# Two elements innermost in place of four in the one-hot operands of a graph kernel's adjacency build

## The reference, cut to what matters

```python
agg = jax.ops.segment_sum(h[src], dst, num_segments=n)       # network 0, three times
z = jax.nn.relu(_batchnorm((h + agg) @ W1[i] + b1[i], g1[i], be1[i])) @ W2[i] + b2[i]
...
summed = jax.ops.segment_sum(x[col], row, num_segments=n)    # network 1: src and dst swapped, mean
msg_sum = jax.ops.segment_sum(x[src], dst, num_segments=n)   # network 2: mean
neigh = jax.ops.segment_max(feat[src] * w[:, None], dst, num_segments=N)   # network 3: maximum, then a weighted mean
```

## Time and profile before

| what | us |
|---|---|
| median of 3 runs | 4930.73 |
| lowest and highest of the 3 | 4900.83, 4937.73 |
| the profiled execution | 4922.53 |
| its span in the profile | 4920.7 |
| PE busy in the span | 3483.8 (71%) |
| DVE busy | 2147.8 (44%) |
| ACT busy | 1956.0 (40%) |
| GpSimd (POOL) busy | 1782.5 (36%) |

### The profile page before, as it was taken

One profiled execution on the slowest core, in us unless ns is written; L12 is line 12 of the kernel. 1 busy time (PEld: TensorE's weight loads), 2 busy tenths in 40 slices (PEclk: granted clock), 3 DMA queues, 4 the chain that ended last, 5 costly groups with the idle time before them and its releaser, 6 DMA issues.

```text
span 4920.7 us, 57973 instructions
## 1 busy us (share of the span) xinstructions
PE 3483.8 (71%) x22119; PEld 2928.1 (60%) x22119; DVE 2147.8 (44%) x4433; ACT 1956.0 (40%) x3073; POOL 1782.5 (36%) x1727
## 2 busy tenths in 40 slices
PE   4899999921112997995118999983477686877678
PEld 2677777611002996994108989973355565665566
DVE  7776676610001986884012233242233333333335
ACT  4677777710000444554005546552222222222221
POOL 3000000077773000777760000005555555556530
PEclk9999999955555998997559989996788898889889
DMA  4878788800002667442004424423255555556555
GB/s 146 228 213 230 214 219 231 240 21 7 7 7 47 223 236 236 151 130 53 4 7 140 133 72 144 130 62 108 71 196 185 193 189 191 188 197 214 170 183 179
DMA packets 299723, 712.84 MB, mean 145 GB/s; under 512 B 65270, under 2 KB 167445, under 8 KB 284214
## 3 DMA queue, kind: packets, MB, share of 16 engines
q1 hardware_dynamic: 167180, 436.77, 27.7%
q10 hardware_dynamic: 52298, 174.64, 9.9%
q0 software_dynamic: 79968, 97.68, 9.2%
HBM read 503.59 MB, written 254.50 MB: 154 GB/s over the span
## 4 chain that ended last, share of the span: by engine, by line
PE 53%; another core or an unknown queue 25%; DVE 7%; issue 6%; ACT 6%; DMA 2%; ACTq 1%; DVEq 0%; SPq 0%
PE PS L740 21%; PE PS L1725 7%; PE PS L662 6%; PE PS L625 5%; PE PS L1711 3%; PE PS L671 2%; PE PS L1701 2%; DMA turned<-DEG 2%; PE PS L1693 2%; DVE BB L1877 2%; ACT DEG L884 1%; PE PS L718 1%; ACT CA L859 1%; DVE PAN L549 1%
## 5 line engine op out<-in xcount | busy, mean ns | idle before, releaser
L431 POOL DMA_INDIRECT PAN<-table,src_i x832 | 826.6, 994 | 1359.1 <-DMA table<-DEG 769.7
L972 POOL DMA_INDIRECT shares<-dst_f,spare x832 | 886.7, 1066 | 738.1 <-ACTq L777 426.8
L740 PE MATMUL PS<-CX,XH 125*128 125x376 f32 x2000 | 477.8, 318 | 261.6 <-issue 181.2
L740 PE MATMUL PS<-CX,XL 125*128 125x376 f32 x2000 | 472.9, 315 | 141.9 <-issue 141.9
L740 PEld LDWEIGHTS PS<-CX,XH 125*128 125x128 f32 x2000 | 321.3, 197 | 279.9 <-issue 219.9
L1819 ACT ACTIVATE BB<-PS 128x1024 f32<-128x1024 f32 x104 | 106.5, 1024 | 938.5 <-PE PS L1701 567.6
L625 PE MATMUL PS<-hot 128*128 128x250 bf16 x1250 | 382.7, 397 | 34.7 <-ACT CA L859 20.3
L537 ACT ACTIVATE CX<-PAN 125x3125 fp32r<-125x3125 uint8 x106 | 298.2, 2815 | 271.1 <-PE PS L740 233.6
L740 PEld LDWEIGHTS PS<-CX,XL 125*128 125x128 f32 x2000 | 321.7, 197 | 141.5 <-issue 141.5
L740 PE MATMUL PS<-CP,XH 125*128 125x376 f32 (+1 forms) x1330 | 310.7, 313 | 120.3 <-DVE XL L1070 63.0
L1701 PE MATMUL PS<-ident,BB 128*128 128x128 f32 x832 | 141.5, 325 | 310.6 <-DVE BB L1877 249.6
(11 more groups left out here) (334 smaller groups left out, 6998.0 us busy)
## 6 DMA issues: line engine op xcount, KB each, us to landing
PAN<-counts SPq DMA_DIRECT2D x300, 390.6 KB
shares<-SSB ACTq DMA_DIRECT2D x70, 1600.0 KB
XP<-shares SPq DMA_DIRECT2D x50, 1600.0 KB
PAN<-shares SPq DMA_DIRECT2D x50, 1600.0 KB
BB<-start_penalty SPq DMA_DIRECT2D x104, 512.0 KB
shares<-blank ACTq DMA_DIRECT2D x15, 3200.0 KB, 13.7
turned<-DEG SPq DMA_DIRECT2D x50, 781.2 KB, 9.3
PAN<-turned SPq DMA_DIRECT2D x100, 390.6 KB
```

The lines of the kernel that those rows point to most:

```text
L431: nc.gpsimd.indirect_dma_start(out=gbuf[g % 2][:, k, :], out_offset=None, in_=source, in_offset=bass.IndirectOffsetOnAxis(ap=src_i[:, t:t ...
L740: last = nc.tensor.matmul(wide_ps[b][h][:, 0:w], halves[part][0:TN, s * SUBJ + j, :], cast_part(v, j, h), start=(s == 0 and j == 0 and par ...
L972: nc.gpsimd.indirect_dma_start(out=shares_flat, out_offset=bass.IndirectOffsetOnAxis(ap=share_at[:, t:t + 1], axis=0), in_=share[:, t:t + ...
```

## The change

`hot_lo` is stored as [2 pairs][128 values][2 windows] in place of [128][4], and `hot_key` as [4 windows][125 values][2 halves] in place of [2][125][4]. The counting table is repeated twice in place of four times. Sizes, instruction counts, waits and order stay as they were; PE reads both operands with a step of two bf16 elements, 4 bytes, and DVE's inputs repeat in runs of two elements.

```diff
-        hot_lo = [hot[:, r * hot_size:r * hot_size + QUAD * 128].rearrange("p (n w) -> p n w", w=QUAD) for r in range(RING)]
-        hot_key = [hot[:, r * hot_size + QUAD * 128:(r + 1) * hot_size].rearrange("p (a n w) -> p a n w", a=2, w=QUAD)
+        hot_lo = [hot[:, r * hot_size:r * hot_size + QUAD * 128].rearrange("p (q n w) -> p q n w", q=2, w=2) for r in range(RING)]
+        hot_key = [hot[:, r * hot_size + QUAD * 128:(r + 1) * hot_size].rearrange("p (w n a) -> p w n a", w=QUAD, a=2)
                    for r in range(RING)]
...
-        iota_h = firsts[:, 0:128 * QUAD].rearrange("p (n w) -> p n w", w=QUAD)
+        iota_h = firsts[:, 0:256].rearrange("p (n w) -> p n w", w=2)
...
-                    keys = hot_key[u % RING][:, i % 2, :, :].rearrange("p n (w a) -> p w a n", w=2)[:, x, :, :]
-                    last = nc.tensor.matmul(pair_ps[n % 2][:, x, :], hot_lo[u % RING][:, :, 2 * (i % 2) + x], keys,
+                    keys = hot_key[u % RING][:, 2 * (i % 2) + x, :, :].rearrange("p n a -> p a n")
+                    last = nc.tensor.matmul(pair_ps[n % 2][:, x, :], hot_lo[u % RING][:, i % 2, :, x], keys,
                                             start=True, stop=True)
...
-            placed_after(dve, nc.vector.tensor_copy(iota_h, iota[:, :].unsqueeze(2).to_broadcast([128, 128, QUAD])))
+            placed_after(dve, nc.vector.tensor_copy(iota_h, iota[:, :].unsqueeze(2).to_broadcast([128, 128, 2])))
...
-                nc.vector.tensor_tensor(out=hot_lo[r], in0=iota_h,
-                                        in1=slot_lo[:, w:w + QUAD].unsqueeze(1).to_broadcast([128, 128, QUAD]),
-                                        op=ALU.is_equal)
-                keys = slot_key[:, 2 * w:2 * w + 2 * QUAD].rearrange("p (a w) -> p a w", a=2)
+                los = slot_lo[:, w:w + QUAD].rearrange("p (q w) -> p q w", q=2)
+                nc.vector.tensor_tensor(out=hot_lo[r], in0=iota_h.unsqueeze(1).to_broadcast([128, 2, 128, 2]),
+                                        in1=los.unsqueeze(2).to_broadcast([128, 2, 128, 2]), op=ALU.is_equal)
+                keys = slot_key[:, 2 * w:2 * w + 2 * QUAD].rearrange("p (w a) -> p w a", w=QUAD)
                 nc.vector.tensor_tensor(out=hot_key[r],
-                                        in0=iota_h[:, 0:TN, :].unsqueeze(1).to_broadcast([128, 2, TN, QUAD]),
-                                        in1=keys.unsqueeze(2).to_broadcast([128, 2, TN, QUAD]),
+                                        in0=iota_h[:, 0:TN, :].unsqueeze(1).to_broadcast([128, QUAD, TN, 2]),
+                                        in1=keys.unsqueeze(2).to_broadcast([128, QUAD, TN, 2]),
                                         op=ALU.is_equal).then_inc(hot_full, 1)
```

## The result

The changed kernel took 4881.49 us on the median of 20 runs (4840.47 to 4909.2), the kernel before 4925.59 (4900.83 to 4960.68). The ratio is 0.9916, 95% interval 0.9898 to 0.9934: 41 us less (33 to 50) where 90 were forecast. The change is a gain, but less than half of the forecast. The median lies inside the range that the prediction gave (4795 to 4890), near its slow end.

What follows compares the result with a forecast made beforehand. PE was taken to bound the build (280 to 944.2 us). Gains of 86 there and 18 before, less 12 for late DMAs and 2 for the scatter's start, gave 90 us: 4930.7 to 4841 us, range 4795 to 4890 (0.81).

Steps and rivals of the forecast that it cites:

- Which engine bounds the build, and what L625 costs: Build: PE bounds it; a 4-byte step takes L625 from 0.22 to 0.11 us a product, 0.22 us less a pair.
- Rival (b): L625: a step of 4 bytes is no faster than 8, or the step wasn't the cause; no gain, 4931 us; chance 0.12.
- VectorE keeps its pairs: DVE's quads: runs of two still let L1168 handle two elements at a time; a quad stays at 1.06 us.
- rival (c): DVE's quads: pairing lost, a quad takes 1.86 us, kernel 57 us slower at 4988 us; chance 0.07.
- L1164 unchanged: DVE: a sign that the forecast is right, L1164 and L1168 keep their durations.
- Odd products, 37: Build's 7 odd products: 43.0 us becomes 37, PE, ACT and DVE coupled by two-buffer rings; gain 6 each (bounds 8.4 and 3).
- Even products, 39.4 and then 1.5 for DMA: Build's 8 even products: 44.9 us becomes 39.4, PE-bound; 1.5 each charged for late turned writes, 12 in all.
- Rival (a), DMA takes over: Build: DMA becomes the bound, even products gain only 1 us each, 66 us in all, 4865 us; chance 0.14.
- The beginning: Before 280 us: slice 0's pairs and products 0 to 3 gain 18 us in sum.
- The 38 pairs of slice 0: Before product 0: a ring of PE, ACT and PE; 0.2 us off each of 19 rounds, 4 us.
- The end: Scatter and everything behind it: starts near 890 us and keeps its length, so the kernel gains what the build gains.
- the DMA backlog: Between build and scatter: the scatter's start at 980.03 us hangs on it; 2 us more charged for a longer one.

Runs made afterwards that it cites:

- Experiment 3: Changed kernel with only the moving operand (the key's one-hot) at a step of two elements, the stationary one still at four; single execution 4854.8 us.
- experiment 7: Changed kernel with five DMAs for each turned tile and the stationary operand (source's one-hot) back in its old layout; 0.9792 of the kernel before, 4833.5 us.
- Experiment 6: Changed kernel with five DMAs for each turned tile, leaving out 831 of 832 edge-weight columns on VectorE (result incomplete); single execution 4810.3 us.
- experiment 1: Changed kernel with each turned tile written in five DMAs in place of one, each fifth waited for by itself; 0.9833 of the kernel before, 4825.7 us.
- experiment 2: Kernel before the change with the same five DMAs for each turned tile, each fifth waited for by itself; 0.9988 of the kernel before, 4896.1 us.
- experiment 5: Changed kernel, one DMA for each turned tile, with each even product's four zero writes moved from steps 10, 20, 30, 40 to 28, 35, 42, 49; single execution 4847.6 us.
- experiment 8: Changed kernel with five DMAs for each turned tile and product 19's three zero writes moved to products 5, 9 and 13; 0.9823 of the kernel before.

## Why the prediction was wrong

**Which engine bounds the build, and what L625 costs.** Right. The 0.44 us of a pair was the moving operand's step of 8 bytes, and 4 bytes cost nothing (a pair takes 0.23 us afterwards). Experiment 3 shows it by the operand alone, and 1250 products went from 402 to 278 ns. Rival (b) is out. The Trainium skill, "SBUF — State Buffer", section "Door 1", would have bf16 steps of 4 elements read free; as TensorE's moving operand they read at half speed here, and the measurement decides.

**VectorE keeps its pairs.** Right for L1168, 672 ns before and after, so rival (c) is out. "L1164 unchanged" was wrong by 67 ns, which experiment 7 shows without effect.

**Odd products, 37.** They came to 38.3, a gain of 4.7 each in place of 6, or 33 us in place of 42. The step named three engines in a ring. Experiment 6 strikes VectorE from it.

**Even products, 39.4 and then 1.5 for DMA: the step that failed.** "More writes are late. I charge 1.5 for each of the 8 even products (bounds 0 and 4.5 each)." The mechanism was the right one, in the right place, but the term measures 6.2, beyond its upper bound. With the late write the 8 even products take 369.4 us (the changed kernel), without it 320.1 (experiment 1), 49 over 8. Their sums, in this order:

```profile
sum 369.42, PE 329.06 PEld 253.84 DVE 254.79 ACT 264.77 POOL 7.34; mean PE 41.13 PEld 31.73 DVE 31.85 ACT 33.10 POOL 0.92
```

```profile
sum 320.13, PE 314.54 PEld 246.71 DVE 254.44 ACT 264.22 POOL 7.32; mean PE 39.32 PEld 30.84 DVE 31.80 ACT 33.03 POOL 0.92
```

ScalarE waits for the write once in each of the 8, 42.5 us together. PE stands 34.8 us longer for it (40.4 beside 5.6), and is busy 14.5 us longer for the same instructions, at the lower clock behind each stall. The forecast had no term for that second part. What it took off for the faster reads was right: 320.1 us is 5.5 a product less than the 364.1 before. The split itself is worth little of it, 2.0 us of these products in experiment 2.

How could it have been sized? That the time to reuse shrinks by 2 us was right (17.5 to 15.3). But the prediction held against it the median landing of 9.3 us and charged an average, while the same write is the slow one in every even product, since the schedule puts it beside the counts write each time. The trace before shows it landing in 15.5, 19.0, 20.2, 16.6 and 20.6 us. Against 15.3 these alone give an estimate of 3.1 us a product, twice the charge. The rest is the write's own slowing and the clock.

**Rival (a), DMA takes over.** It forecast 4865 by way of a full DMA. The time came nearer to it than to the forecast, but experiments 1 and 5 show that capacity wasn't short: the same bytes fit when they are waited for later or issued elsewhere.

**The beginning.** The first four products and what is before them gained 6.1 us in place of 18. The 38 pairs of slice 0 gained 0.8 (PE's first L662 at 89.0 in place of 89.9) in place of 4: the ring's round hardly shrank. Product 0 gained 5.6 beside a forecast of 5. Then product 1 grew from 57.2 to 62.2 and took it back. Its first copy into the tile CA waits until the counts write of slice 0 has landed, before and after the change:

```profile
140.32 1.16 ACT L859 ACTIVATE CA<-PS 128x500 bf16<-128x500 f32 x2 [3.11 <-DMA counts<-CA]
```

```profile
139.42 1.16 ACT L859 ACTIVATE CA<-PS 128x500 bf16<-128x500 f32 x2 [8.83 <-DMA counts<-CA]
```

Product 1 starts 6.4 us sooner and gets going 0.9 us sooner. Product 2 gained 0.5 in place of 5, with a wait of 3.9 for a `turned` write; in experiment 1 it takes 41.2, the 5 us. Product 3 gained 4.2.

**The end.** Product 19 and the scatter's start moved with the build (35.8 to 35.6), and the gain of the build reached the end as forecast: 34 us at the scatter beside 41 (33 to 50) in the time, and in experiment 1 92 beside 82 (63 to 101). The forecast's reason for the gap between build and scatter, the DMA backlog, was mostly wrong (experiment 8).

The sum, then: 27.7 us from products 4 to 18 in place of 74, and 6 from the first four in place of 18. Without late writes (experiment 1) the scatter came 92 us sooner where the forecast without its DMA charges said 104. That 92 is near the 90 of the forecast is luck: the 15 us missing there in the odd products and the beginning, less 3 gained in product 19, happen to come near the 14 charged for DMAs, of which hardly any is left.

## What to carry to other kernels

When a bound engine gets faster, go through the waits that it is just in time for today, one place of the schedule at a time: for each buffer that a DMA frees, compare that DMA's own landing time with the new time to reuse. Take the landing time from the kernel before as a lower bound: here it grew by 1 to 5 us. Splitting such a write into parts that are waited for one by one nearly doubles its slack at no cost in memory (here 0.9916 became 0.9833), for five times as many DMAs. Moving unrelated bulk writes away from it freed the even products as well, but can put them in the way of what comes later. An operand that TensorE streams ran at full rate here with neighbouring bf16 columns 4 bytes apart and at half of it with 8; for the operand that it loads as weights it didn't matter.

## What the runs showed of the hardware that was not expected

- A step of 8 bytes in a bf16 moving operand halves TensorE's rate (0.88 ns a column at the 2.4 GHz level); one of 4 bytes costs nothing (a pair shows 0.23 us in the chain above, 0.46 ns a column). The stationary operand's step changed its load from 113 to 100 ns.
- After PE had stood for 6.4 us in the middle of a busy stage, its clock was at the 1.2 GHz level from 382.9 to about 388.5 us. Over the 8 even products 34.8 us of longer standing brought 14.5 us of slower work, some 0.4 as much again.
- A write of 781 KB whose landing takes 6.6 us at best took 19.1 to 22.6 us in every even product, 3 us behind a counts write and with zero writes behind it; with the first zeros issued later it took 15.3 (experiment 5), at a DMA share below 1 in both.
- The VectorE instruction with a counting table repeated in its outer dimension and numbers in runs of two took 547 ns on the median where the one with runs of four took 480, for 512 elements; for 1000 elements both took 672. Why isn't known.
- The part behind the scatter's start isn't steady from one profiled execution to the next: 3940.7 us before, 3925.1 in the changed kernel, between 3908 and 3963 in the eight experiments, which hardly change anything there. By these spans a single execution of a variant can be off by 25 us either way (an estimate). The cuts by product are steadier: in the four kernels with finer writes and the changed key (1, 6, 7, 8) each of products 4 to 18 repeats within 0.5, product 1 within 1.1.
